# Pair preparation: norm by thirds, squares on ScalarE, pads and a power of -0.5 on GpSimd

## The reference

```python
def _rmsnorm(x, w):
    xf = x.astype(jnp.float32)
    y = xf * jax.lax.rsqrt(jnp.mean(xf * xf, axis=-1, keepdims=True) + EPS)
    return y.astype(x.dtype) * w
HD = 2                                  # 32 heads of two features
qkv = x @ w_qkv.T                       # x = _layernorm(h)
q, k, v = jnp.split(qkv, 3, axis=-1)
q = _rmsnorm(heads(q), qn_w)
k = _rmsnorm(heads(k), kn_w)
att = jnp.einsum('bhtd,bhsd->bhts', q, k) * scale
```

## Time and profile before

| | us |
|---|---|
| median of 3 runs | 1406.91 |
| lowest, highest run | 1406.87, 1408.58 |
| profiled execution, its own time | 1405.85 |
| its span, first to last instruction | 1404.1 |

### The profile page before, as it was taken

How to read it: one execution, slowest core, us unless ns; L and a number is a source line. 1 busy time by engine, 2 the same in 40 slices (tenths; PEclk the granted TensorE clock), 3 DMA queues, 4 the chain that set the end, 5 groups by cost and what they waited for, 6 DMA issues and landing times. The chain is left out here.

```text
span 1404.1 us, 27705 instructions
## 1 busy us (share of the span) xinstructions
PE 1075.7 (77%) x11369; PEld 609.2 (43%) x11369; DVE 905.2 (64%) x1932; ACT 763.8 (54%) x1071; POOL 166.3 (12%) x177
## 2 busy tenths in 40 slices
PE   5667974562879969935999999988799999997240
PEld 3456953351534444431333333354455556555220
DVE  0476547867891277775675555454799999984524
ACT  0452322221207643358999999932489898982020
POOL 0005402310002200000000000010024000000524
PEclk9788976765659979976999999978899999998575
DMA  7100000021000000000000000010000000002021
GB/s 148 29 1 1 4 4 17 0 35 43 3 1 1 1 0 1 1 2 3 1 2 1 1 1 1 2 29 14 1 2 2 2 3 3 2 2 68 13 46 27
DMA packets 42817, 18.23 MB, mean 13 GB/s; under 512 B 38069, under 2 KB 41641, under 8 KB 42437
## 3 DMA queue, kind: packets, MB, share of 16 engines
q1 hardware_dynamic: 40965, 15.39, 5.2%
q0 software_dynamic: 1728, 1.08, 0.4%
HBM read 12.95 MB, written 3.48 MB: 12 GB/s over the span
## 5 line engine op out<-in xcount | busy, mean ns | idle before, releaser
L2481 ACT ACTIVATE pt_PT<-ps 128x1024 f32<-128x1024 f32 x288 | 266.1, 1107 | 5.9 <-PE ps L2551 5.6
L3473 DVE TENSOR_SCALAR da_AD<-da_QH,da_XG,da_XH 128x1024 f32<-128x1024 f32 x296 | 231.3, 850 | 16.1 <-PE ps L3630 15.3
L3521 ACT ACTIVATE da_AD<-ps,da_NX 128x1024 f32<-128x1024 f32 x214 | 220.9, 1182 | 29.7 <-PE ps L3630 29.3
L3630 PE MATMUL ps<-da_AD,dw_win 128*32 128x256 f32 x4080 | 230.7, 382 | 4.6 <-DVE da_AD L3473 2.3
L3630 PEld LDWEIGHTS ps<-da_AD,dw_win 128*32 128x32 f32 x4080 | 130.2, 110 | 102.4 <-DVE da_AD L3473 15.1
L2517 PE MATMUL ps<-pt_PT,pa_V 128*32 128x512 f32 (+3 forms) x1536 | 155.5, 499 | 8.3 <-DVE pt_Yc L2458 3.2
L2465 DVE TENSOR_TENSOR pt_PT<-pt_PT,pt_keep 128x512 f32<-128x512 f32 x128 | 84.3, 689 | 61.2 <-ACT pt_PT L2481 60.1
L2551 PE MATMUL ps<-pt_QT,pt_KT 12*128 12x512 bf16 (+3 forms) x768 | 80.1, 334 | 3.2 <-DVE pt_KT L2423 0.5
L2517 PEld LDWEIGHTS ps<-pt_PT,pa_V 128*32 128x32 f32 x1536 | 38.9, 109 | 64.8 <-issue 63.6
L2090 ACT ACTIVATE mt_act<-ps 128x342 f32<-128x342 f32 (+1 forms) x66 | 30.1, 455 | 54.4 <-PE ps L2145 54.4
L2145 PE MATMUL ps<-mt_XF,ew_w 64*128 64x342 f32 (+1 forms) x132 | 54.6, 498 | 0.8 <-ACT mt_WT L2076 0.8
(11 more groups left out here) (789 smaller groups left out, 2053.0 us busy)
## 6 DMA issues: line engine op xcount, KB each, us to landing
em_xs<-in_x_dram SPq DMA_DIRECT2D x2, 1152.0 KB, 9.5
em_xs<-in_x_dram SPq DMA_DIRECT2D x2, 1024.0 KB, 13.8
cp_xbuf<-ci_zero SPq DMA_DIRECT2D x1, 672.0 KB
cp_XS<-cp_xbuf SPq DMA_DIRECT2D x8, 84.0 KB, 2.3
cp_ybuf<-cp_YS SPq DMA_DIRECT2D x8, 84.0 KB, 2.1
ew_win<-in_L_ffn_w_dram SPq DMA_DIRECT2D x2, 320.0 KB
em_WS<-in_L_tok_W_dram SPq DMA_DIRECT2D x8, 72.0 KB
la_blk<-la_scratch SPq DMA_DIRECT2D x8, 64.1 KB
```

Of the source, the lines that this page charges most:

```text
L2481: nc.scalar.activation(PT[:, n % RING, 2 * i:2 * i + 2, :], ps[:, b0:b0 + 2, :], ACT.Exp, scale=SCALE).then_inc(exp_ok, 1)
L3473: nc.vector.tensor_scalar(AD[:, j % RING], QH[:, b], XG[:, b, s:s + 1], XH[:, b, s:s + 1], ALU.max, ALU.subtract).then_inc(ad_dve, 1)
L3521: nc.scalar.activation(AD[:, j % RING], QA, ACT.Abs, bias=NX[:, b, s:s + 1]).then_inc(ad_act, 1)
L3630: ins = nc.tensor.matmul(o, D.win[:, int(by[j] == "D"), hp, 15 - m:47 - m], AD[:, j % RING, hp], start=False, stop=False, skip_group_check ...
```

## The change

On VectorE, the layer norm is cut into thirds of six tiles: `centre(q)` (sum, mean, difference), `variance(q)` and `rows_out(q)` (reciprocal and product), in the order centre 0, centre 1, variance 0, centre 2, rows 0, variance 1, rows 1, variance 2, rows 2. The square between difference and variance moves to ScalarE, and so does the square in `means`, which ScalarE now takes from PSUM beside the copy of q and k. TensorE transposes a third as soon as it is there, between units. The pads of Q12 and K12 are filled by GpSimd behind V1. The root and the reciprocal of the means become one GpSimd instruction for each group, a tensor_tensor with the operation pow whose second operand is a tile of -0.5.

A square stood before each reduction, and a reciprocal before the four scaling instructions. The diff:

```diff
@@ -2189,13 +2189,12 @@
         XL = sb("XL", [64, 2, 128])
         sq = sb("sq", [128, T, 128])
         pm = sb("pm", [128, T, 64])
-        zero = sb("zero", [128, 1])
-        qkw = sb("qkw", [128, 2, 2])
+        qkw, minus = sb("qkw", [128, 2, 2]), sb("minus", [128, 6])
...
@@ -2211,22 +2210,57 @@
 
             @block.gpsimd
             def _(pool):
-                nc.gpsimd.memset(zero[:], 0.0).then_inc(zero_ok, 1)
+                nc.gpsimd.memset(minus[:], -0.5)
                 nc.gpsimd.memset(V1[:], 1.0).then_inc(ones_ok, 1)
+                for k, a in enumerate((Q12, K12)):
+                    pool.wait_ge(ones_ok, k + 1)
+                    nc.gpsimd.memset(a[:].rearrange("p t h e -> p (t h) e").bitcast(F32)[:, :, 6:16], 0.0
+                                     ).then_inc(ones_ok, 1)
+                for c, (t, n) in enumerate(GROUPS):
+                    pool.wait_ge(m_ok, c + 1)
+                    nc.gpsimd.tensor_tensor(pm[:, t:t + n], pm[:, t:t + n], minus[:].unsqueeze(2).to_broadcast([128, n, 64]),
+                                            ALU.pow).then_inc(r_ok, 1)
 
             @block.vector
             def _(dve):
                 link = Chain(dve, chain)
                 tt = nc.vector.tensor_tensor
-                layernorm_dve(nc, dve, link, K.h[:], xn[:], tmp[:], st[:], var_ready, std_ready)
-                nc.vector.tensor_copy(st[:, 0, :], st[:, 3, :]).then_inc(x_ok, 1)
+                third = lambda q: slice(6 * q, 6 * q + 6)
+
+                def centre(q):
+                    s = third(q)
+                    link(nc.vector.tensor_reduce(st[:, 0, s], K.h[:, s], AX.X, ALU.add))
+                    link(nc.vector.tensor_scalar(st[:, 0, s], st[:, 0, s], 1.0 / 64, None, ALU.mult))
+                    tt(xn[:, s], K.h[:, s], bcl(st[:, 0, s], 64), ALU.subtract).then_inc(xc_ok, 1)
+
+                def variance(q):
+                    s = third(q)
+                    dve.wait_ge(xsq_ok, q + 1)
+                    link(nc.vector.tensor_reduce(st[:, 1, s], tmp[:, s], AX.X, ALU.add))
+                    nc.vector.tensor_scalar(st[:, 1, s], st[:, 1, s], 1.0 / 64, 1e-5, ALU.mult, ALU.add
+                                            ).then_inc(var_ready, 1)
+
+                def rows_out(q):
+                    s = third(q)
+                    dve.wait_ge(std_ready, q + 1)
+                    link(nc.vector.reciprocal(st[:, 3, s], st[:, 2, s]))
+                    tt(xn[:, s], xn[:, s], bcl(st[:, 3, s], 64), ALU.mult).then_inc(x_ok, 1)
+
+                centre(0)
+                centre(1)
+                variance(0)
+                centre(2)
+                rows_out(0)
+                variance(1)
+                rows_out(1)
+                variance(2)
+                rows_out(2)
                 dve.wait_ge(c_in, 64)
 
                 def means(c):
                     t, n = GROUPS[c]
                     g = slice(t, t + n)
                     dve.wait_ge(qkv_sb, 3 * c + 3)
-                    link(tt(sq[:, g], qk[:, g], qk[:, g], ALU.mult))
                     link(nc.vector.tensor_reduce(pm[:, g], sq[:, g].rearrange("p t (h e) -> p t h e", e=2),
                                                  AX.X, ALU.add))
                     nc.vector.tensor_scalar(pm[:, g], pm[:, g], 0.5, 1e-6, ALU.mult, ALU.add).then_inc(m_ok, 1)
@@ -2235,7 +2269,6 @@
                     t, n = GROUPS[c]
                     g = slice(t, t + n)
                     dve.wait_ge(r_ok, c + 1)
-                    link(nc.vector.reciprocal(pm[:, g], pm[:, g]))
                     for a in range(2):
                         v = half(qk, t, n, 64 * a)
                         for e in range(2):
@@ -2269,39 +2302,47 @@
 
             @block.scalar
             def _(act):
-                def pads(dst):
-                    f = dst[:].rearrange("p t h e -> p (t h) e").bitcast(F32)[:, :, 6:16]
-                    nc.scalar.copy(f, zero[:].unsqueeze(2).to_broadcast([128, 512, 10]))
-
-                act.wait_ge(zero_ok, 1)
-                pads(Q12)
-                root_act(nc, act, st[:], var_ready, std_ready)
+                def square(q):
+                    act.wait_ge(xc_ok, q + 1)
+                    nc.scalar.activation(tmp[:, 6 * q:6 * q + 6], xn[:, 6 * q:6 * q + 6], ACT.Square).then_inc(xsq_ok, 1)
+
+                def root(q):
+                    act.wait_ge(var_ready, q + 1)
+                    nc.scalar.activation(st[:, 2, 6 * q:6 * q + 6], st[:, 1, 6 * q:6 * q + 6], ACT.Sqrt
+                                         ).then_inc(std_ready, 1)
+
+                def rows_in(q):
+                    for g in (2 * q, 2 * q + 1):
+                        act.wait_ge(tr_ps, g + 1)
+                        nc.scalar.copy(XT[:, g * GRP:(g + 1) * GRP], ps[0:64, g, 0:GRP]).then_inc(tr_sb, 1)
+
+                square(0)
+                square(1)
+                root(0)
+                square(2)
+                root(1)
                 act.wait_ge(wt_ps, 1)
                 nc.scalar.copy(WT[:], ps[0:64, 7, 0:192]).then_inc(wt_sb, 1)
                 nc.scalar.copy(wpT[:], ps[0:64, 7, 192:256]).then_inc(wt_sb, 1)
-                for g in range(NG):
-                    act.wait_ge(tr_ps, g + 1)
-                    nc.scalar.copy(XT[:, g * GRP:(g + 1) * GRP], ps[0:64, g, 0:GRP]).then_inc(tr_sb, 1)
-                act.wait_ge(tr_sb, NG)
-                last = XT[:].rearrange("p (b t) -> p b t", b=2)[:, :, SEQ - 1:SEQ]
-                nc.scalar.copy(XL[:], last.to_broadcast([64, 2, 128])).then_inc(last_sb, 1)
+                rows_in(0)
+                root(2)
                 act.wait_ge(ones_ok, 1)
 
-                def roots(c):
-                    t, n = GROUPS[c]
-                    act.wait_ge(m_ok, c + 1)
-                    nc.scalar.activation(pm[:, t:t + n], pm[:, t:t + n], ACT.Sqrt).then_inc(r_ok, 1)
-
                 for u in range(9):
+                    if u == 2:
+                        rows_in(1)
+                    if u == 5:
+                        rows_in(2)
+                        act.wait_ge(tr_sb, NG)
+                        last = XT[:].rearrange("p (b t) -> p b t", b=2)[:, :, SEQ - 1:SEQ]
+                        nc.scalar.copy(XL[:], last.to_broadcast([64, 2, 128])).then_inc(last_sb, 1)
                     act.wait_ge(qkv_ps, u + 1)
                     both = ps[:, (6 + u) % 8, 0:384].rearrange("p (t c) -> p t c", t=2)
                     nc.scalar.copy(V1[:, 2 * u:2 * u + 2, 0:96].rearrange("p t (h e) -> p t h e", e=3)[:, :, :, 0:2],
                                    both[:, :, 128:192].rearrange("p t (h e) -> p t h e", e=2))
+                    nc.scalar.activation(sq[:, 2 * u:2 * u + 2, :], both[:, :, 0:128], ACT.Square)
                     nc.scalar.copy(qk[:, 2 * u:2 * u + 2, :], both[:, :, 0:128]).then_inc(qkv_sb, 1)
-                    if u in (5, 8):
-                        roots(u // 3 - 1)
-                roots(2)
-                pads(K12)
+                act.wait_ge(ones_ok, 3)
                 for c in range(3):
                     t, n = GROUPS[c][0], split(c)
                     act.wait_ge(rest_ok, c + 1)
@@ -2320,10 +2361,20 @@
                 for i in range(3):
                     nc.tensor.transpose(ps[0:64, 7, 64 * i:64 * i + 64], W3[:, i], K.ident[0:64, 0:64])
                 nc.tensor.transpose(ps[0:64, 7, 192:256], wp[:], K.ident[0:64, 0:64]).then_inc(wt_ps, 1)
-                pe.wait_ge(x_ok, 1)
-                transposes(nc, K, lambda t: xn[:, t], P, 64, tr_ps)
+
+                def rows_in(q):
+                    pe.wait_ge(x_ok, q + 1)
+                    for g in (2 * q, 2 * q + 1):
+                        for j in range(3):
+                            ins = nc.tensor.transpose(ps[0:64, g, j * P:(j + 1) * P], xn[:, 3 * g + j],
+                                                      K.ident[0:P, 0:P])
+                        ins.then_inc(tr_ps, 1)
+
+                rows_in(0)
                 pe.wait_ge(wt_sb, 2)
                 for u in range(9):
+                    if u in (2, 5):
+                        rows_in(u // 2)
                     if u < 8:
                         pe.wait_ge(tr_sb, ((u // 4) * PADSEQ + 256 * (u % 4) + 255) // GRP + 1)
                     else:
```

More of the change, by code:

```diff
@@ L2191, in pairs_prepare @@
         pm = sb("pm", [128, T, 64])
-        zero = sb("zero", [128, 1])
-        qkw = sb("qkw", [128, 2, 2])
+        qkw, minus = sb("qkw", [128, 2, 2]), sb("minus", [128, 6])
         c_in, chain, var_ready, std_ready = sem("c_in"), sem("chain"), sem("var"), sem("std")
+        xc_ok, xsq_ok, inv_ok = sem("xc_ok"), sem("xsq_ok"), sem("inv_ok")
         x_ok, wt_ps, wt_sb, tr_ps, tr_sb, last_sb = (sem("x_ok"), sem("wt_ps"), sem("wt_sb"), sem("tr_ps"),
                                                      sem("tr_sb"), sem("last_sb"))
-        qkv_ps, qkv_sb, ones_ok, zero_ok, m_ok, r_ok = (sem("qkv_ps"), sem("qkv_sb"), sem("ones"), sem("zeros"),
```

(2 more changed lines are left out.)

## The result

| | before | after |
|---|---|---|
| time, median of 4 runs each | 1406.89 us (1401.12 to 1408.58) | 1575.88 us (1572.11 to 1578.77) |
| ratio, 95% interval | | 1.1175 (1.1141 to 1.1209) |
| profiled execution, time and span | 1405.85, 1404.1 us | 1576.96, 1575.2 us |
| mean granted TensorE clock | 0.848 | 0.809 |
| GpSimd busy | 166.3 us, 12% | 360.4 us, 23% |

A forecast was written before the change was run, and what follows sets the result against it. The stage was bound by a chain of mostly VectorE work, for which TensorE waits. Its end at 637.3 + 3P, P = 4.6, gave 651.1, 6.8 us later: 1405.85 to 1412.7, plus 1.06 for the median, 1413.7; range 1400 to 1437.

The forecast's parts named there:

- P: Time of one GpSimd power of 384 columns in the means, three in the stage; taken as 4.6 us.
- one factor: For the power: VectorE's reciprocal against its subtraction, 2.55/0.55 = 4.6 times, which gave P = 4.6 us.
- the dear power: Rival for the means: P over 8, to 13.7 us, +17 to +34 us, up to 1441; chance 0.19.
- The bound from above: Upper limit for one power: logarithm, product and exponential, 3 x 4.6 x 0.99 = 13.7 us.
- The code-fetch rival: Code is first fetched for the power: 1.28 us once, 1415; about 6 us by the skill, 1419.7; chance 0.03.
- my sum: Stage's end at 637.3 + 3P, from the first means on, the three powers never overlapping VectorE's work.
- the lock rival: VectorE goes on during fills and powers; powers back to back, end at 634.4, 9.9 us sooner, 1397.0; chance 0.17.
- Its tail: In the lock rival: three powers back to back, then 5.34 us from the third scaling to the stage's end.
- the forecast's own front: Stage up to the first means: first third ready at 615.3, first mean starting at 621.5, done at 622.8.
- a unit of products: TensorE's products between transposes and first mean: 5.46/8 = 0.7 us a unit.

The follow-up runs named there:

- e1: The changed kernel with ScalarE's root and VectorE's reciprocal put back instead of the power: 1414.68 us, ratio to before 1.0011.
- e2: The kernel before with only the GpSimd power in place of root and reciprocal: 1579.94 us in one run.
- e3: The kernel before with powers and one product added on scratch tiles in GpSimd's idle time of the pair attention: 1405.77 us in one run.
- e5: The changed kernel without the power, VectorE's short norm scalars replaced by a product with a 1/64 tile and ScalarE's root: 1406.65 us, ratio to before 0.9954.
- e10: e5 with VectorE's first scaling ahead of the second means and ScalarE's first root right behind the fourth unit: 1404.19 us, ratio to before 0.9925.

## Why the prediction was wrong, point by point

**The term that failed is P.** It was right that the three powers lie one after the other on the path, so that the end moves by three times P; e1 and e2 show that the loss comes with the power and goes with it. The size was not: P was 4.6 us as worked out from one factor and is 61.5 us as measured, 13 times as much, and that makes the sum wrong by 171 us. No rival held it either: the dear power ended at 13.7, and the range at a P of 12.3.

**The bound from above was no bound.** It took a power as three functions, each as dear, against a product, as VectorE's reciprocal is against VectorE's subtraction. That is a ratio between two of VectorE's operations, and it said nothing of a routine on GpSimd. No row of the trace of before priced any function of many steps on GpSimd; the rows of its products gave its cost for one simple operation and were right for that (1.01 us in e3, 0.99 in the earlier trace rows). e3 shows that the power is not in that family: 160 ns a column against 2.1. With P unpriced and multiplied by three, the upper end should have stayed open, and the range should have said so.

The estimate in the prediction from "GPSIMD Engine Reference", section 3.1, of the Trainium skill (about 12 cycles an element where code branches on its data) was 3.8 us a power. The measured 61.5 is 16 times that, and the measurement decides. The code-fetch rival is out: the first power started 0.08 us behind the scalar that it waits for (624.69) and took 61.57 us, the others 61.52 and 61.51, so that what was paid only once is at most 0.06 us there.

**The second step that failed: the casts did not wait for the power.** I had seen VectorE's scalars wait for fills, and took it that casts wait for any GpSimd instruction. So my sum lets GpSimd and VectorE take turns and adds VectorE's work to 3P. In the trace the casts ran in 0.36 and 0.35 us inside a power, the powers followed each other without a gap, and VectorE's work between them was hidden. Only the first of the four scaling instructions lost time, 0.58 us where a power started beside it. So the lock rival was half right: fills held VectorE's scalars, powers did not. Its tail behind the forecast's own front fits with the true P: first mean done at 622.9, and 622.9 + 3 x 61.52 + 5.34 = 812.8, against a measured end of 814.71, less the 0.41 by which the stage starts later, 814.3; nearly all of the difference is the later first mean, below. My own sum, 637.3 + 3P, would have been 821.9, 7.6 too much. With the P of 4.6 that I took, the same tail ends at 642.0 (an estimate), where the forecast had 651.1 and the kernel before 644.28. So the direction was right by luck: at that P the step turned a small gain into a loss, and by this sum the change is slower only because P is above 5.3. The Trainium skill's "SBUF — State Buffer", in "Who interferes with whom", says that copies, casts and tensor_scalars can enter a mode in which they contend with GpSimd, and that whoever issues first then has the shared ports for its whole instruction. The fills agree (ends 0.03 us apart); the power does not, and the measurement decides.

**The front of the stage was right.** The scalars were forecast to end at 604.1, 608.6 and 613.0 and ended, less the 0.41 of the later start, at 604.1, 608.6 and 613.0. A pad's fill was forecast at 4.3 us and 0.1 and took 4.37. The first third was forecast 13.2 us into the stage; its transposes started at +12.47, with the last product in front of them ending 0.06 us earlier. The subtraction and the reduction passed the fills, the squares and the table load were hidden, and no configuration was loaded for the power.

**A term was missing: TensorE's clock.** The first mean came at 623.34, less the shift 622.93, and was forecast at 621.5. I took 0.7 us for a unit of products from the earlier trace rows, where the clock had gone to full. The changed kernel ran its first eight matmuls in 2.89 us, 1.4 a unit, all at 0.50: 1.4 us at the first mean. e3 shows the same with the code of before: the row that I had read was one that another execution need not repeat. In before's stage it is worth 3.6 us, more than the 2.8 us that I had set as what a measurement can tell.

**What stays open.** The order of the ratios follows the stage, but the times fell more than it did: against e3's stage e5 is 3.9 us shorter and e10 6.8, and their medians are 6.7 and 9.1 us under those of before. The intervals of the ratios, 4.1 to 8.8 and 7.1 to 14.1 us, leave the stage's own gain just outside, and e3 itself is one run. A sign lies in the clock averaged over a whole run: its median is 0.841 for the runs of before and 0.844 to 0.845 for those of e5 and e10, and over the 61 runs of before beside the experiments a time is on average 7.8 us shorter for each 0.01 more of that clock. So the rest may be TensorE's clock in other stages; no run shows it. Why a power costs the same for 2 partitions as for 128 was not taken apart either. Another way to the power, a logarithm and an exponential on ScalarE, was not run.

## What to carry to other kernels

An operation that no row of the trace prices is first measured by itself, on an engine that idles at that time and beside an unchanged path; e3 did it in one run. Do not carry a ratio between two operations from one engine to another, and where such an unknown is multiplied by a count, leave the range open at that end. Long GpSimd fills beside VectorE's small scalars give away what a pipelined start gains: cut the fills, or give the scalars a form with two inputs, and then fill VectorE's remaining wait by order.

## What the hardware showed beyond what I had expected

- GpSimd's power costs 160 ns a column, 61.5 us for 384, whether 2, 16 or 128 partitions take part, with the exponents -0.5 and 1 and the bases 2 and 1 alike (15.65 to 15.89 us for 96 columns); a product of the same shape costs 1.01 us.
- A power leaves VectorE's copy-like instructions alone (a cast in 0.36 us within it), while a fill of 4.37 us makes a scalar of 6 elements wait for its end (3.34 us). A two-input instruction lost 0.58 us where a power started beside it, and nothing inside a fill; in the router of before one lost 0.6 us just behind the start of a GpSimd tensor_scalar (0.94 against 0.33), and the next, inside the same instruction, nothing.
- The same code had TensorE at the full clock in this stage in one profiled execution (before) and at half in another (e3), 3.6 us apart at the next part.
